# Attention with experts on one core: value products in twos, rows copied by ScalarE and divided by GpSimd, sums of four blocks held

## The reference

```python
Q = (x @ Wq.T).reshape(H, b, s, dkh)      # H = 16, b = 4, s = 1024, dkh = 16
K = (x @ Wk.T).reshape(H, b, s, dkh)
V = (x @ Wv.T).reshape(H, b, s, dvh)
scores = jnp.einsum('hbqd,hbkd->hbqk', Q, K)
atten = jax.nn.softmax(scores, axis=-1)
out = jnp.einsum('hbqk,hbkd->hbqd', atten, V).reshape(b, s, -1)
y = out + x
mu = jnp.mean(y, axis=(1, 2), keepdims=True)
var = jnp.var(y, axis=(1, 2), keepdims=True)
return (y - mu) / jnp.sqrt(var + EPS)
```

## Time and profile before

| | |
|---|---|
| median of 3 runs | 1015.22 us (1014.22 to 1015.4) |
| profiled execution | 1013.82 us, span 1011.7 us |
| TensorE busy | 986.7 us (98%) |
| VectorE busy | 800.3 us (79%) |
| ScalarE busy | 678.7 us (67%) |
| GpSimd busy | 175.7 us (17%) |
| chain that ended last | TensorE 91%, ScalarE 3%, VectorE 2% |
| granted TensorE clock | 0.995 of full speed over the span |

### The profile page before, as it was taken

One profiled execution on the slowest core, in us unless ns is written; L12 is line 12 of the kernel. 1 busy time (PEld: TensorE's weight loads), 2 busy tenths in 40 slices (PEclk: granted clock), 3 DMA queues, 4 the chain that ended last, 5 costly groups with the idle time before them and its releaser, 6 DMA issues.

```text
span 1011.7 us, 20754 instructions
## 1 busy us (share of the span) xinstructions
PE 986.7 (98%) x7816; PEld 520.6 (51%) x7816; DVE 800.3 (79%) x1023; ACT 678.7 (67%) x1355; POOL 175.7 (17%) x325
## 2 busy tenths in 40 slices
PE   7999999999998999999999999999999999999995
PEld 6888888888876333333334333343333333333332
DVE  4343455533466899999999999999999999999967
ACT  2312333343322788888888888888888888888884
POOL 2001445444455100000000000000000000000000
PEclk9999999999999999999999999999999999999997
DMA  9967442223300233333333333333333333432204
GB/s 357 367 239 221 134 143 73 73 76 95 106 3 1 63 88 96 90 88 96 87 95 91 93 91 91 94 84 96 90 92 94 85 95 90 95 90 71 72 18 167
DMA packets 127043, 108.59 MB, mean 107 GB/s; under 512 B 81120, under 2 KB 102368, under 8 KB 126944
## 3 DMA queue, kind: packets, MB, share of 16 engines
q1 hardware_dynamic: 122720, 102.81, 35.2%
q10 hardware_dynamic: 4224, 4.46, 1.3%
HBM read 80.75 MB, written 42.21 MB: 122 GB/s over the span
## 4 chain that ended last, share of the span: by engine, by line
PE 91%; ACT 3%; DVE 2%; issue 2%; DMA 1%; POOL 1%; SPq 0%; ACTq 0%; POOLq 0%; DVEq 0%
PE ps L1037 26%; PE ps L1017 22%; PE ps L970 18%; PE ps L1002 10%; PE ps L923 6%; PE ps L895 4%; PE ps L911 2%; ACT wp L554 2%; PE ps L1048 1%; PE ps L1060 1%; DMA qf<-ot 1%; PE ps L884 1%; DMA wp<-w_out_t 1%; ACT vstage L554 1%; DVE xn L854 0%
## 5 line engine op out<-in xcount | busy, mean ns | idle before, releaser
L713 DVE TENSOR_REDUCE negm<-ps 128x1 f32<-128x1024 f32 x512 | 615.6, 1221 | 24.3 <-PE ps L1002 14.9
L554 ACT ACTIVATE wp<-ps 128x512 f32<-128x512 f32 x680 | 367.4, 603 | 35.7 <-PE ps L1017 3.9
L1017 PE MATMUL ps<-qf,kf 50*128 50x512 f32 x1024 | 385.1, 452 | 0.3 <-DMA qf<-ot 0.2
L1002 PE MATMUL ps<-kf,qf 48*128 48x512 f32 x1024 | 361.8, 445 | 0.9 <-DVE negm L713 0.9
L1017 PEld LDWEIGHTS ps<-qf,kf 50*128 50x128 f32 x1024 | 158.7, 184 | 202.7 <-ACT wp L554 107.7
L1037 PE MATMUL ps<-wp,vb 128*17 128x256 f32 x2720 | 212.6, 385 | 0.3 <-issue 0.2
L1002 PEld LDWEIGHTS ps<-kf,qf 48*128 48x128 f32 x1024 | 144.0, 185 | 4.3 <-issue 3.9
L554 ACT ACTIVATE picks<-ps 128x512 f32<-128x512 f32 x172 | 103.6, 603 | 17.9 <-PE ps L1017 1.8
L704 DVE SCALAR_TENSOR_TENSOR acc<-ps,gates,acc 128x256 f32<-128x256 f32 x64 | 30.7, 480 | 99.2 <-PE ps L970 94.8
L1037 PEld LDWEIGHTS ps<-wp,vb 128*17 128x17 f32 x2720 | 46.0, 95 | 118.8 <-ACT vstage L554 49.4
L554 ACT ACTIVATE vstage<-ps 128x512 f32<-128x512 f32 x172 | 103.7, 603 | 1.1 <-PE ps L1017 1.1
(11 more groups left out here) (117 smaller groups left out, 836.7 us busy)
## 6 DMA issues: line engine op xcount, KB each, us to landing
qk_d<-stage SPq DMA_DIRECT2D x64, 256.0 KB
feat_d<-qk_d SPq DMA_DIRECT2D x64, 256.0 KB, 3.3
qf<-feat_d SPq DMA_DIRECT2D x128, 128.0 KB
qf<-feat_d SPq DMA_DIRECT2D x128, 64.0 KB
kf<-feat_d SPq DMA_DIRECT2D x128, 64.0 KB
v_d<-vstage ACTq DMA_DIRECT2D x8, 544.0 KB, 5.1
vb<-v_d SPq DMA_DIRECT2D x128, 34.0 KB, 2.3
acc<-x SPq DMA_DIRECT2D x8, 512.0 KB, 6.9
```

The lines of the kernel that those rows point to most:

```text
L554: nc.scalar.activation(weight_tile(n, j, b)[:, h * HALF:(h + 1) * HALF], ps[:, ST_BANK[(2 * unit + b) % 3], :], ACT.Exp).then_inc(exp_done, 1)
L713: nc.vector.tensor_reduce(negm[:, n % 2, qt:qt + 1], ps[:, b:b + 2, :].rearrange("p b c -> p (b c)"), AX.X, ALU.max, negate=True).then_inc ...
L1002: last = nc.tensor.matmul(ps[:, MAX_BANK[turn % 2] + half, :], qf[rows, u, qt * P:(qt + 1) * P], kf[rows, u, :], start=True, stop=True)
L1017: nc.tensor.matmul(ps[:, ST_BANK[(2 * unit + half) % 3], :], kf[rows, u, j * P:(j + 1) * P], qf[rows, u, h * HALF:(h + 1) * HALF], start=T ...
```

## The change

- TensorE: behind the first unit of a step (h = 0) no value product is issued, behind the second (h = 1) two.
- `ot` holds the sums of four blocks (HELD = 4) in place of two. The copy of block n waits for the R that read block n - 4.
- The rows of a pair of blocks: ScalarE copies R's 128 x 272 numbers out of the bank (`copy_rows`) behind the last exponential of the second step; GpSimd takes the reciprocal as a power of -1, multiplies, and adds to the tokens. VectorE does this as before only for the last pair. The turn that R used is then free on `rows_copied`; `served` counts the turns that VectorE still frees.
- To make room, several small tiles share one tile `choice`, and the constant `onesm` is written later, over `gates`.

```diff
+    HELD = 4
...
-        ot = sb("ot", [P, 6, 2, TB])
+        ot = sb("ot", [P, 6, HELD, TB])
...
+        rows = choice[:, 0:16 * VW].rearrange("p (g c v) -> p g c v", g=4, c=4)
+        minus = sb("minus", [P, 4, 4])
...
+        copied_turns = [row_turn[pair] for pair in range(NB // 2 - 1)]
+
+        def served(turn):
+
+            return turn + 1 - sum(row <= turn for row in copied_turns)
...
             def residual(pair):
-                pool.wait_ge(turn_done, row_turn[pair] + 1)
-                nc.gpsimd.tensor_tensor(xn[:, bass.ds(pair, 1), :].rearrange("p o d -> p (o d)"),
-                                        xn[:, bass.ds(pair, 1), :].rearrange("p o d -> p (o d)"),
-                                        att[:], ALU.add).then_inc(y_done, 1)
...
+                pool.wait_ge(rows_copied, pair + 1)
+                nc.gpsimd.tensor_tensor(rden[:], rows[:, :, :, DH], minus[:], ALU.pow).then_inc(rows_step, 1)
+                pool.wait_ge(rows_step, 2 * pair + 1)
+                nc.gpsimd.tensor_tensor(rows[:, :, :, 0:DH], rows[:, :, :, 0:DH],
+                                        rden[:].unsqueeze(3).to_broadcast([P, 4, 4, DH]), ALU.mult).then_inc(rows_step, 1)
+                pool.wait_ge(rows_step, 2 * pair + 2)
+                tile = xn[:, bass.ds(pair, 1), :].rearrange("p o (c g d) -> p (o g) c d", c=4, g=4)
+                nc.gpsimd.tensor_tensor(tile, tile, rows[:, :, :, 0:DH], ALU.add).then_inc(y_done, 1)
...
-                if n >= 2:
-                    act.wait_ge(turn_ready, row_turn[n // 2 - 1] + 1)
-                nc.scalar.copy(ot[:, 0:groups, n % 2, :], ps[:, PV_BANK, 0:groups * TB].rearrange("p (g t) -> p g t", t=TB)
+                if n >= HELD:
+                    act.wait_ge(turn_ready, row_turn[(n - HELD) // 2] + 1)
+                nc.scalar.copy(ot[:, 0:groups, n % HELD, :], ps[:, PV_BANK, 0:groups * TB].rearrange("p (g t) -> p g t", t=TB)
                                ).then_inc(pv_evac, 1)
+
+            def copy_rows(pair):
+                turn = row_turn[pair]
+                act.wait_ge(turn_ready, turn + 1)
+                if pair:
+                    act.wait_ge(y_done, pair)
+                nc.scalar.copy(rows, ps[:, MAX_BANK[turn % 2], :].rearrange("p (g c v) -> p g c v", g=4, c=4)[:, :, :, 0:VW]
+                               ).then_inc(rows_copied, 1)
...
+                    if j == LAG - 1 and n % 2 == 1 and n > 1:
+                        copy_rows((n - 3) // 2)
...
                     if n % 2 == 1 and n > 1:
-                        if qt == 2 * LAG - 1:
-                            normalise((n - 3) // 2)
-                        elif qt == NKT - 1:
+                        if qt == NKT - 1:
                             statistics((n - 3) // 2)
...
                 if turn >= 2:
-                    pe.wait_ge(turn_done, turn - 1)
+                    if turn - 2 in copied_turns:
+                        pe.wait_ge(rows_copied, copied_turns.index(turn - 2) + 1)
+                    else:
+                        pe.wait_ge(turn_done, served(turn - 2))
...
-                        if j >= LAG:
-                            sum_values(n, j - LAG, h)
-                        elif n:
-                            sum_values(n - 1, NKT // 2 + j - LAG, h)
+                        for b in range(2 * h):
+                            if j >= LAG:
+                                sum_values(n, j - LAG, b)
+                            elif n:
+                                sum_values(n - 1, NKT // 2 + j - LAG, b)
```

More of the change, by code:

```diff
@@ L97, in attention_and_experts @@
         gates = sb("gates", [P, NT, E])
[L98 to L105, removed]
+        onesm = gates[:].rearrange("p t e -> p (t e)")[:, 0:P]
+        top1, top2, first, gap, ex, gs, g1, g2 = (choice[:, NT * (E + i):NT * (E + i + 1)] for i in range(8))
         wp = sb("wp", [P, 4, POS])
@@ L197, in attention_and_experts @@
         rden_done = sem("rden_done")
+        rows_copied = sem("rows_copied")
+        rows_step = sem("rows_step")
         y_done = sem("y_done")
         ystat_done = sem("ystat_done")
+        means_const = sem("means_const")
         fin_d = sem("fin_d")
@@ L327, in max_rows @@
                     first = half * ROWS + FR
-                    sp.dma_start(qf[first:first + 2, slot, :].bitcast(FP32), ot[0:2 * NKT, 4:6, par, :]
+                    sp.dma_start(qf[first:first + 2, slot, :].bitcast(FP32), ot[0:2 * NKT, 4:6, n if n < 2 else (n - 2) % HELD, :]
                                  ).then_inc(mrow_in[slot], 16)
@@ L367, in _ @@
             nc.gpsimd.memset(ident[:], 0.0).then_inc(const_step, 1)
-            nc.gpsimd.memset(onesm[:], 1.0 / P).then_inc(const_step, 1)
-            for value, tile in ((-0.5, mhalf), (EPS, epst), (0.0, zero)):
+            for value, tile in ((-0.5, mhalf), (EPS, epst), (0.0, zero), (-1.0, minus)):
                 nc.gpsimd.memset(tile[:], value).then_inc(const_step, 1)
@@ L403, in residual @@
             def residual(pair):
-                pool.wait_ge(turn_done, row_turn[pair] + 1)
-                nc.gpsimd.tensor_tensor(xn[:, bass.ds(pair, 1), :].rearrange("p o d -> p (o d)"),
-                                        xn[:, bass.ds(pair, 1), :].rearrange("p o d -> p (o d)"),
-                                        att[:], ALU.add).then_inc(y_done, 1)
+                tile = xn[:, bass.ds(pair, 1), :].rearrange("p o d -> p (o d)")
+                if pair == NB // 2 - 1:
+                    pool.wait_ge(turn_done, served(row_turn[pair]))
+                    nc.gpsimd.tensor_tensor(tile, tile, att, ALU.add).then_inc(y_done, 1)
+                    return
+                pool.wait_ge(rows_copied, pair + 1)
[6 more added lines that the diff above has]
+                nc.gpsimd.tensor_tensor(tile, tile, rows[:, :, :, 0:DH], ALU.add).then_inc(y_done, 1)
             def max_halves(n):
                 par = n % 2
-                pool.wait_ge(turn_done, max_turn[n, NKT - 1] + 1)
+                pool.wait_ge(turn_done, served(max_turn[n, NKT - 1]))
                 if n in (2, 3):
@@ L428, in _ @@
                     max_halves(1)
+            pool.wait_ge(ff_sum, NT)
+            nc.gpsimd.memset(onesm, 1.0 / P).then_inc(means_const, 1)
             for n in range(2, NB):
@@ L725, in normalise @@
                 dve.wait_ge(turn_ready, turn + 1)
+                dve.wait_ge(y_done, pair)
                 nc.vector.reciprocal(rden[:], o[:, :, :, DH]).then_inc(rden_done, 1)
[L727 to L730, removed]
+                dve.wait_ge(rden_done, 1)
+                nc.vector.tensor_tensor(att.rearrange("p (c g d) -> p g c d", c=4, g=4), o[:, :, :, 0:DH],
                                         rden[:].unsqueeze(3).to_broadcast([P, 4, 4, DH]), ALU.mult
@@ L848, in _ @@
             for c in range(EARLY * NC // BATCH):
[L849 to L851 removed]
+                if c == BATCH:
                     statistics(NB // 2 - 2)
@@ L1048, in to_token_rows @@
                     last = nc.tensor.transpose(ps[:, MAX_BANK[turn % 2], g * P:(g + 1) * P],
-                                               ot[:, g].rearrange("p b t -> p (b t)"), ident[:])
+                                               ot[:, g, 2 * pair % HELD:2 * pair % HELD + 2].rearrange("p b t -> p (b t)"), ident[:])
                 last.then_inc(turn_ready, 1)
@@ L1069, in mean_over_partitions @@
                     pe.wait_ge(fin_d, 7 * part + 4)
-                    nc.tensor.matmul(ps[:, MEAN_BANK[1], 0:n], onesm[:], dev2[:, entries], start=True, stop=True
+                    nc.tensor.matmul(ps[:, MEAN_BANK[1], 0:n], onesm, dev2[:, entries], start=True, stop=True
                                      ).then_inc(fin_pe, 1)
```

15 lines of the change are left out of this document (8 added, 7 removed).

## The result

| | us | of the kernel before |
|---|---|---|
| before, median of 5 runs | 1014.53 (1013.52 to 1015.4) | |
| changed, median of 5 runs | 1067.16 (1065.72 to 1068.11) | ratio 1.0519, 95% interval 1.0507 to 1.0531 |
| changed, profiled execution | 1066.44, span 1064.5 | |

The forecast was 1065, with a range of 1044 to 1087. The change makes the kernel 5.2% slower, by the mechanism that was forecast.

What follows compares the result with a forecast made beforehand. The prediction took TensorE's own order to bound the kernel. From the profiled 1013.8 us, 31.75 periods of 1.63 added 51.8 and the end gave back 0.7: 1064.9, predicted as 1065, range 1044 to 1087.

Steps and rivals of the forecast that it cites:

- R: TensorE's row transposes, once in two blocks, in odd blocks; with T they put the next score 0.65 us behind T.
- The pair: Two units in attention blocks: the fourth score waits for the first exponential, so a pair takes 2.59 us against 2.44.
- The saving: Two units grouped on TensorE would take 2.13 us instead of 2.44 if nothing waited, 0.31 less.
- T: TensorE's transposes of the maxima in the middle of a block, forecast 2.59 us after the second pair's first score.
- The middles: Middle of each block, around the transposes: 0.71 us lost in even blocks, 1.08 in odd ones.
- The other edits: VectorE's relief worth nothing in blocks; GpSimd's 4.5 us chain costs nothing, at 5.6 us it costs 6 us.
- The cover: Time in blocks before VectorE's statistics need GpSimd's sum: VectorE free at 9.3, 5.4 us of GpSimd's chain covered.
- the usual 1.63 per period: Extra time per two blocks, 22.51 us against 20.88; over 31.75 periods +51.8 us.
- VectorE's lateness: At the kernel's end VectorE normalised the last rows 0.77 us late; forecast to be given back, -0.7 us.
- rival 2: GpSimd's chain decides: from 5.4 us each microsecond costs up to 31 us; 1099 at 6.5; chance 0.06.
- Rival 1: TensorE's switches decide, the fourth score needn't wait, VectorE is next: 1.6 us less per period, about 965; chance 0.09.
- Rival 3: Saving and wait cancel: 2.39 us per pair, two blocks 20.9, time stays at 1015; chance 0.03.

Runs made afterwards that it cites:

- Run 5: The changed kernel with one of each unit's two products for maxima left out, scores still in three banks: 1066.84 us, ratio 1.0512 to the kernel before.
- run 6: The changed kernel with one of each unit's two products for maxima left out and its bank given to scores as a fourth: 959.31 us, ratio 0.9450.
- Run 9: The changed kernel with one product for maxima per unit left out, three score banks, and exponentials of 256 of 512 columns: 999.9 us, ratio 0.9855.
- Run 7: The kernel before, old order, with one product for maxima per unit left out and a fourth bank for scores: 1003.94 us, ratio 0.9886.
- Run 2: The changed kernel with the old order of value products, so all other edits alone: 1013.9 us, ratio 0.9990 to the kernel before.
- run 1: The kernel before with only the order changed, two value products behind every second unit: 1073.47 us, ratio 1.0583.
- run 4: The changed kernel with exponentials of only 256 of each score tile's 512 columns: 1012.86 us, ratio 0.9990 to the kernel before.

## Why the prediction was right

**The pair.** The forecast chain 0.54 + 0.60 + 0.06 + 0.43 + 0.43 + 0.56 reads 0.53 + 0.60 + 0.05 + 0.43 + 0.99 in the changed kernel, where the trace shows the two value products as one row. 2.602 was measured for 2.59. Runs 5 and 6 show the cause: with the fourth bank the pair is 2.13 and the kernel is 107.5 us faster. Run 9 shows it from the other end: an exponential shorter by 0.22 (in the mean 0.61, then 0.39) shortens the pair by the same 0.22 (2.606, then 2.387).

**The saving.** 2.13 for a pair without the wait was right too: run 6 has 2.132, though with three products in a unit in place of four, so it tests the order and not each term. Run 7, with the same three products in the old order, has 1.223 per unit: the saving is 2 x 1.223 - 2.132 = 0.31, as forecast. The rule of the Trainium skill, "TensorEngine Tiling (Array Packing)", section "Key Properties", that a change of tiling mode drains the engine, agrees with the four banks' rows: 0.44 from value product to value product, 0.54 from there to T. No run shows the drain apart from other things that could make up these 0.10. Its warning in "PSUM Bottleneck", that emptying the results doesn't get faster with tiling, points to the right engine but not to the reason. ScalarE's pace isn't the limit: it is busy for 493.63 of 632 us, and with whole exponentials and four banks the pair takes 2.13. It is the wait for one exponential, which three banks put into the chain.

**The middles.** 0.71 was forecast for even blocks; with the measured pair the fences give 5.89 - 2 x 2.60 = 0.69. For odd blocks 1.08 was forecast, and 6.19 - 5.20 = 0.99 measured. The mis-sized term is ScalarE's copy of the rows: it holds the next exponential back by 0.26 (616.43, 616.69), where I took the 0.37 of the longer copy. In the period, 22.50 for 22.51, this and the 0.01 per pair cancel.

**The other edits.** The power of 16 elements takes 2.90 to 2.91 us for 2.84, the chain 4.46 (rows copied at 616.82, sum done at 621.28) for 4.5. On the clock of the pair before T, VectorE came to its statistics at 9.24 (621.84 - 612.60) for 9.3, which is 0.56 after the sum was done. The cover held in the blocks: no statistics waited for GpSimd there. Run 2 shows these edits at -0.1% in the old order; run 1, which leaves them out, shows that together they are worth 6 us in the new one.

**Where the sum is off.** In the spans, from the start to the first R it is +2.11 (365.65, 367.76; forecast 1.5 x 1.63 = 2.4), over the 29 periods +46.95 (forecast 47.3), to the last R +3.25 (27.28 us from 971.15 to 998.43 in the earlier trace rows, 30.53 from 1020.21 to 1050.74; forecast 1.25 x 1.63 = 2.0), and behind that +0.5 (forecast -0.7). The first two came out a little under the forecast, the last two each 1.2 over it, so that the sum lies nearer than its parts:
- The last two blocks have no products for maxima for later blocks. Where these are missing, units of the old order are shorter than 1.22, but a new pair is as long as ever, since the chain through the three banks doesn't contain them. I had charged the usual 1.63 per period; from the row transposes of 971.15 and 1020.21 to the next ones (990.82 and 1042.60) the new order takes 22.39 and the old 19.67, 2.72 more. Value products there, first of the kernel before (two units take 2.17), then of the changed one (a pair takes 2.60):

```profile
987.11 0.63 PE L1037 MATMUL ps<-wp,vb 128*17 128x256 f32 x8
...
989.28 0.63 PE L1037 MATMUL ps<-wp,vb 128*17 128x256 f32 x8
```

```profile
1033.80 1.06 PE L1060 MATMUL ps<-wp,vb 128*17 128x256 f32 x16
...
1036.40 0.63 PE L1060 MATMUL ps<-picks,vb 128*17 128x256 f32 x8
```

- At the end I had forecast that VectorE's lateness goes. It grew, since its statistics waited 3.09 us for GpSimd (1048.36), and the work queued behind them ended 1.26 us after the last rows were there. It is rival 2, at one place of the kernel. In blocks VectorE had reductions to do meanwhile; here it had none.

**The rivals.** Rival 1 (switches decide) holds in four banks, where a pair takes the 2.13 us that the switches gave; in three banks it is hidden. That its 965 us lies near the 959 of run 6 is chance: 965 was worked out from VectorE's 2.25 us per pair, and run 6 lets VectorE reduce half the columns. Its period of 19.01 is 8 x 2.13 and 1.95 for the middles. Rival 2 costs about a microsecond in all, at the end (+0.5 where -0.7 was forecast). Rival 3 would have needed a pair of 2.39; only a shorter exponential brought one (run 9).

## What to carry to other kernels

Work that is grouped to save an engine's switches makes its results come in bursts: count the banks that a burst needs before you count the switches. If the ring is one bank short, the burst waits for a whole chain (first result to reader's start, the reader's length, release, reload), and that chain, worked out from rows of the old order, gave the new pair to 1%. A step that cost nothing while its reader had slack, like the copies on ScalarE, is to be priced anew as soon as that reader is in the chain.

## What the runs showed that I had not expected

- The next wait behind the banks of scores: with half the exponential, the two turns of maxima hold most pairs at 2.43 us or more, though VectorE's work per pair is 2.25 (run 4). Its total did not show that; the moment at which each turn is asked for did.
- With four banks (run 6) VectorE waits 26.8 us for GpSimd's sum, in 28 of the periods, up to 1.0 each, and TensorE's scores wait 28.3 us for the DMAs that bring the copied maxima to the queries. The cover for GpSimd's chain, 0.56 us in the changed kernel, is gone for two reasons: two blocks take 19.0 us in place of 22.5, and VectorE's shorter reductions bring it to the statistics earlier. Run 5, with the shorter reductions at 22.51, already has 11.1 us of this wait, 0.5 at most.
- ScalarE starts an exponential 0.26 us after a copy that takes 0.39 (616.43, 616.69), and the sums' copy of 0.48 holds the next back by 0.37: what a copy costs in this queue is the distance to the next start, a good 0.1 less than its length.
